# Adapter with layer norm: residual copied into PSUM by ScalarE, up-bias added by one product a tile

## What is computed

```python
h = x @ W_down[e] + b_down[e]        # 512x512 times 512x256
h = gelu(h)                          # exact gelu
h = h @ W_up[e] + b_up[e]            # 512x256 times 256x512
h = x + h                            # the residual
out = (h - mean) / sqrt(var + 1e-5) * ln_w[e] + ln_b[e]
```

## Time and profile before

| | |
|---|---|
| median of 3 runs | 68.33 us (67.98 to 68.78) |
| the profiled execution | 67.71 us |
| its span, first to last instruction | 65.8 us |
| TensorE busy | 57.7 us (88%) |
| VectorE busy | 49.6 us (75%) |
| ScalarE busy | 34.8 us (53%) |
| GpSimd busy | 40.3 us (61%) |
| DMA moved | 14.75 MB, mean 224 GB/s |

### The profile page before, as it was taken

How to read it: one execution, slowest core, us unless ns; L and a number is a source line. 1 busy time by engine, 2 the same in 40 slices (tenths; PEclk the granted TensorE clock), 3 DMA queues, 4 the chain that set the end, 5 groups by cost and what they waited for, 6 DMA issues and landing times. The chain is left out here.

```text
span 65.8 us, 975 instructions
## 1 busy us (share of the span) xinstructions
PE 57.7 (88%) x300; PEld 48.1 (73%) x300; DVE 49.6 (75%) x95; ACT 34.8 (53%) x51; POOL 40.3 (61%) x43
## 2 busy tenths in 40 slices
PE   0999999999999999999999999999999999990000
PEld 0999446898888888868888888888999898870000
DVE  0059912539999998969989894499999979999910
ACT  0700299987897559999940729991056204040000
POOL 4000070794999389999998999999199002327300
PEclk9999999999999999999999999999999999999996
DMA  0899897069999999999995074300000752400750
GB/s 0 319 329 309 309 351 289 10 173 420 274 354 416 423 411 339 414 415 411 413 426 217 17 306 179 157 10 0 0 0 0 319 214 105 159 0 0 258 194 26
DMA packets 4468, 14.75 MB, mean 224 GB/s; under 512 B 496, under 2 KB 496, under 8 KB 4464
## 3 DMA queue, kind: packets, MB, share of 16 engines
q1 hardware_dynamic: 4176, 13.65, 54.8%
q10 hardware_dynamic: 288, 1.05, 4.2%
HBM read 10.50 MB, written 4.19 MB: 223 GB/s over the span
## 5 line engine op out<-in xcount | busy, mean ns | idle before, releaser
L214 POOL TENSOR_TENSOR x_lo<-x_raw,x_hi 128x512 fp32r<-128x512 f32 x10 | 13.2, 1346 | 1.0 <-ACT x_hi L274 1.0
L535 PE MATMUL y_ps<-wu_hi,hid_hi 128*128 128x512 f32 x32 | 13.4, 418 | 0.0
L230 POOL TENSOR_TENSOR rstd<-var_eps,minus_half 128x2 f32<-128x2 f32 (+1 forms) x10 | 6.4, 639 | 10.5 <-DVE var_eps L373 10.5
L541 PE MATMUL y_ps<-wu_hi,hid_lo 128*128 128x512 f32 x32 | 12.7, 397 | 0.0
L537 PE MATMUL y_ps<-wu_lo,hid_hi 128*128 128x512 f32 x32 | 12.5, 392 | 0.0
L365 DVE BATCH_NORM_STATS2 stats<-y_ps 128x6 f32<-128x512 f32 x16 | 10.9, 691 | 2.1 <-PE y_ps L541 1.9
L225 POOL TENSOR_TENSOR wu_lo<-w_raw,wu_hi 128x512 fp32r<-128x512 f32 x8 | 10.4, 1321 | 2.1 <-ACT wu_hi L284 2.1
L382 DVE SCALAR_TENSOR_TENSOR y_ps<-y_ps,mean_var,ln_gb 128x512 f32<-128x512 f32 x16 | 11.5, 750 | 0.0
L392 DVE SCALAR_TENSOR_TENSOR result<-y_ps,rstd,ln_gb 128x512 f32<-128x512 f32 x15 | 10.8, 742 | 0.3
L292 ACT ACTIVATE x_res<-x_raw,w_raw 128x512 f32<-128x512 f32 x16 | 10.2, 711 | 0.0
L520 PE MATMUL y_ps<-ident,x_res 128*128 128x128 f32 x64 | 8.6, 272 | 0.0
(11 more groups left out here) (35 smaller groups left out, 87.4 us busy)
## 6 DMA issues: line engine op xcount, KB each, us to landing
x_raw<-x_cols SPq DMA_DIRECT2D x6, 512.0 KB, 7.7
out<-result SPq DMA_DIRECT2D x6, 512.0 KB, 3.0
w_raw<-weights SPq DMA_DIRECT2D x4, 512.0 KB, 7.4
ln_gb<-ln_rows SPq DMA_DIRECT2D x4, 512.0 KB, 12.5
w_raw<-weights SPq DMA_DIRECT2D x3, 516.0 KB, 8.8
x_raw<-x_cols ACTq DMA_DIRECT2D x2, 512.0 KB, 4.1
out<-result SPq DMA_DIRECT2D x4, 256.0 KB, 2.4
w_raw<-weights SPq DMA_DIRECT2D x1, 260.0 KB, 3.6
```

The source lines that it names most:

```text
L214: nc.gpsimd.tensor_tensor(x_lo[:, b % 2, k, :], x_raw[:, b, k, :], x_hi[:, b % 2, k, :].bitcast(F32), ALU.subtract).then_inc(x_lo_done, 1)
L535: nc.tensor.matmul(y_ps[:, t, :], hid_hi[:, p, j, rows], wu_hi[:, p, j, :], start=False, stop=False, skip_group_check=True)
L541: last = nc.tensor.matmul(y_ps[:, t, :], hid_lo[:, p, j, rows], wu_hi[:, p, j, :], start=False, stop=(j == JT - 1), skip_group_check=True)
```

## The change

In batches 1 to 3 the residual no longer goes through TensorE. x comes a second time, with tokens on the partitions (`x_rows`, 1 MB a batch), into the place where a batch's x before lay (`rows_of(b)` is `x_raw[:, b - 1]`), and ScalarE copies it tile by tile into `y_ps` (`copy_rows`), after VectorE's finish of the tile of the batch before. TensorE then waits for `copied`. Batch 0 keeps its way.

b_up is no longer added to x there. Its rows for batches 1 to 3 are loaded twice into partitions 0 to 2 and 3 to 5 of `bias_raw` (by SyncE, two rows of 2 KB each, three times). VectorE makes `bias_parts` of it once (`split_bias`): the rounded value in rows 0 to 2, what is left in rows 3 to 5. GpSimd builds `pick`, a matrix that is one in rows b - 1 and b + 2 for batch b, ScalarE rounds it (`pick_r`), and TensorE adds one product of 128 rows and 512 columns to each tile (12 in all).

```diff
+            def copy_rows(b, t):
+                act.wait_ge(rows_in[b], DMA)
+                act.wait_ge(norm_done, TT * (b - 1) + t + 1)
+                nc.scalar.activation(y_ps[:, t, :], rows_of(b)[:, t, :], ACT.Copy).then_inc(copied, 1)
...
+            def split_bias():
+
+                dve.wait_ge(bias_in, COPIED * DMA)
+                nc.vector.tensor_copy(bias_hi[:], bias_raw[:]).then_inc(bias_hi_done, 1)
+                dve.wait_ge(bias_hi_done, 1)
+                dve.wait_ge(mask_done, 1)
+                nc.vector.scalar_tensor_tensor(out=bias_parts[:], in0=bias_hi[:].bitcast(F32),
+                                               scalar=minus_if_low[:, 0:1], in1=bias_raw[:], op0=ALU.mult,
+                                               op1=ALU.add).then_inc(bias_parts_done, 1)
...
-            def up(b, t, j):
+            def up(b, t, j, low=True):
                 p = b % 2
                 rows = slice(t * P, (t + 1) * P)
                 n = JT * b + j + 1
+                if b and j == 0:
+
+                    pe.wait_ge(copied, TT * (b - 1) + t + 1)
...
+                if b and j == 0:
+                    if (b, t) == (1, 0):
+                        pe.wait_ge(pick_r_done, 1)
+                        pe.wait_ge(bias_parts_done, 1)
+                    nc.tensor.matmul(y_ps[:, t, :], pick_r[:, b - 1, :], bias_parts[:],
+                                     start=False, stop=False, skip_group_check=True)
...
+                if b == 0:
+                    for t in range(TT):
+                        place_residual(t)
+                up(b, 0, 0)
+                up(b, 1, 0)
+                up(b, 0, 1, low=False)
+                up(b, 1, 1, low=False)
+                up_low(b, 0, 1)
+                up_low(b, 1, 1)
```

More of the change, by code:

```diff
@@ L95, in conditional_adapter_kernel @@
         ln_in = [sem(f"ln_in{b}") for b in range(B)]
+        rows_in = [None] + [sem(f"rows_in{b}") for b in range(1, B)]
+        bias_in = sem("bias_in")
+        bias_filled = sem("bias_filled")
         stored = [[sem(f"stored{b}{c}") for c in range(2)] for b in range(LAST)]
@@ L181, in _ @@
             load_wu(0)
-            load_x(1, 0)
-            load_x(1, 1)
+            for b in range(1, 3):
+                load_x(b, 0)
+                load_x(b, 1)
             _, others = nc.values_load_multi_w_load_instructions(
@@ L186, in _ @@
             expert.extend(others)
-            for b in range(1, B):
[L188 to L195, removed]
+            load_wd(1)
+            load_wu(1)
+            load_ln(0)
+            load_wd(2)
+            load_rows(1)
+            for b in range(1, B):
+                load_bias(b)
+            load_wu(2)
+            load_ln(1)
+            load_x(3, 0)
+            load_x(3, 1)
+            load_rows(2)
+            load_wd(3)
+            load_wu(3)
+            load_ln(2)
+            load_ln(3)
+            store(0)
+            load_rows(LAST)
+            for b in range(1, LAST):
                 store(b)
@@ L317, in _ @@
                                  ACT.Copy).then_inc(first_wd_hi_done, 1)
-            residual(0)
+            residual()
             hi_wu(0)
@@ L402, in _ @@
             for b in range(LAST):
[L403 to L410, removed]
+                tile_stats(b, 0)
+                tile_stats(b, 1)
+                moments(b, 0)
+                moments(b, 1)
+                shift_var(b, 0, 2)
+                centre(b, 0)
+                centre(b, 1)
+                tile_stats(b, 2)
+                tile_stats(b, 3)
+                moments(b, 2)
+                moments(b, 3)
+                shift_var(b, 2, 4)
+                finish(b, 0)
+                finish(b, 1)
+                if b == 0:
+                    split_bias()
                 if b + 1 < LAST:
-                    finish(b, 0)
-                    finish(b, 1)
                     lo_hidden(b + 1, 0)
-                    finish(b, 2)
-                    finish(b, 3)
+                else:
+                    lo_hidden_half(0, 0)
+                    lo_hidden_half(0, 1)
+                centre(b, 2)
+                centre(b, 3)
+                finish(b, 2)
+                if b + 1 < LAST:
                     lo_hidden(b + 1, 1)
                 else:
[L419 to L423, removed]
                     lo_hidden_half(1, 0)
-                    finish(b, 3)
+                finish(b, 3)
             for t in range(TT):
```

117 lines of the change are left out of this document (85 added, 32 removed).

## The result

The changed kernel takes 70.62 us (median of 4 runs, 70.16 to 70.91); the kernel before took 68.20 us beside it (4 runs, 67.98 to 68.78). The ratio is 1.0335, with a 95% interval of 1.0248 to 1.0422: slower, by 2.4 us. The forecast was 69.5 us with a range of 67.5 to 71.2. The sign was right and the time lies in the range, but it lies above the span that the forecast gave itself (68.8 to 70.2). The loss is twice what the forecast had, and about half of it comes from a place where the forecast had nothing.

The account below looks back on a forecast made before the run. TensorE and VectorE were taken as nearly level, VectorE alone bounding the tail. Profiled: 67.71 + 2.1 (held split) - 0.8 - 0.1 (given back) = 68.9; as median 68.33 + 1.2 = 69.5 us, range 67.5 to 71.2.

Parts of the forecast that it names:

- held split: VectorE between batches 0 and 1: both split_bias instructions wait for GpSimd subtractions, batch 1's statistics start 2.1 us late.
- TensorE's part: Residual placement: 0.44 us a tile gives way to a 0.23 us bias product, saving 0.21 us a tile, 2.5 us in all.
- the tail: End of the last batch: VectorE has 9.77 us of its own work, so TensorE's savings there cannot move the end.
- ScalarE's part: Twelve copies into PSUM replace twelve residual activations at 0.65 us each; the new order hides the longer chain.
- rival of slow copies: ScalarE's copies into PSUM take 0.9 us or more, TensorE waits for `copied` every tile, past 70 us; chance 0.04.
- rival of the bare price: VectorE is not held in split_bias, which costs only its bare time: 67.6 to 68.4 us; chance 0.22.
- late-bias rival: Bias comes after 25.26 or x's rows late, split_bias misses a GpSimd boundary, term 3.4 us: 70.8 us; chance 0.26.
- The loads: SyncE's queue: W_down 1 goes out at 13.4, x 1's rows arrive at 24.7, the bias 24.8 to 25.2, just in time.
- the signs that the forecast named: Cast ending after a GpSimd subtraction, L486 1.5 us or more, `bias_parts` wait 1 us or more, statistics near 31.3 and 43.3.

Follow-up runs that it names:

- experiment 1: The kernel before with only the two loads of batch 2's x issued ahead of the expert-number load: 69.42 us, ratio 1.0150 to the kernel before.
- experiment 9: The changed kernel with split_bias's rounded copy written to PSUM instead of SBUF: 69.17 us, ratio 1.0135 to the kernel before.
- experiment 11: The changed kernel with all four expert numbers read at SyncE's start and the rounded bias written to PSUM: 68.53 us, ratio 1.0071 to the kernel before.
- experiment 6: The changed kernel with only all four expert numbers read at SyncE's start: 69.90 us, ratio 1.0298 to the kernel before.
- experiment 5: The changed kernel with expert numbers read at the start, bias loads and split_bias moved early, batch 2's x loaded later: 68.02 us, ratio 1.0019 to the kernel before.
- experiment 4: The kernel before with only the new instruction orders of VectorE and TensorE: 68.56 us, ratio 1.0032 to the kernel before.
- experiment 7: The kernel before with all four expert numbers read at SyncE's start: 68.86 us, too spread for a ratio.
- experiment 8: The kernel of experiment 5 with the next batch's W_down rounded behind the second gelu instead of ahead: 68.24 us, ratio 1.0054 to the kernel before.
- Experiment 12: The changed kernel with ScalarE reading the first expert number and issuing early loads, SyncE reading all four, rounded bias in PSUM: 67.97 us, runs 66.45 to 72.07.

## Why the prediction was right in sign and half in size

The ledger between medians: the kernel before 68.2; late loads about +1.2 (experiment 1); held split about +1.4 (experiments 9 and 11); together 70.8. Measured: 70.6. Everything else of the change (cheaper placements less the two bare instructions) comes out near nothing, -0.2 us, less than these runs can tell. The hold's share is measured in the changed kernel itself, twice. The share of the late loads is measured only by putting them into the kernel before; taking them out of the changed kernel (experiment 6) leaves their size open.

**TensorE's part, right in time, too large in busy time.** A tile's residual no longer takes TensorE's time, and the bias product is followed by the next after 0.23 us (31.36 to 31.59 below), as forecast. The timeline of TensorE's products in batch 1:

```profile
30.05 0.47 PE L642 MATMUL y_ps<-bias_parts,pick_r 128*128 128x512 f32 x1 [1.27 <-DVE bias_parts L486]
...
31.13 0.39 PE L636 MATMUL y_ps<-wu_lo,hid_hi 128*128 128x512 f32 x1
31.36 0.39 PE L642 MATMUL y_ps<-bias_parts,pick_r 128*128 128x512 f32 x1
31.59 0.39 PE L654 MATMUL y_ps<-wu_hi,hid_lo 128*128 128x512 f32 x1
```

The forecast gave back 0.8 us between the statistics of batches 1 and 2, and 0.1 behind; measured 0.81, then 0.21 and 0.11 (a total of 1.13 where 0.9 stood). The busy time fell by 1.8 us, not by the 2.5 forecast; no run says where the other 0.7 went. Most of TensorE's saving buys nothing, as the tail said: VectorE's last 9.77 us became 9.66.

**ScalarE's part, right.** The copies, whose price no row before showed, were put at 0.65 us. The page has them at 602 ns:

```profile
L366 ACT ACTIVATE y_ps<-x_raw 128x512 f32<-128x512 f32 x12 | 7.1, 602 | 4.1 <-DVE result L476 4.0
```

The rival of slow copies (0.04) falls. That the chain finish, copy, product costs nothing is borne out by experiment 5, which keeps it and is level with the kernel before; experiment 4 shows that the new orders alone cost nothing that can be told.

**The held split, right in mechanism and nearly in size.** The forecast gave 2.98 us from the end of the first finishes to the next low part (24.47 to 27.45) and 2.1 us at batch 1's statistics; measured 2.71 us (27.12 to 29.83) and 1.71. Both are 0.3 to 0.4 us below the forecast. Experiments 5 and 9 took the hold away, each in its own manner, and found 0.5 to 0.7 and 0.75 us for the two instructions. The Trainium skill, SBUF — State Buffer, "Who interferes with whom", had said that a cast too can be held; the trace of before did not show it, and now 1.10 and 1.12 us beside GpSimd against 0.42 to 0.43 alone do. The rival of the bare price (0.22) is refuted. The late-bias rival (0.26) had nearly the right time, 70.8, for a wrong reason: in the profile VectorE did not wait for the bias at all.

**The loads, the step that failed.** The forecast wrote: "their issue took 0.91 us, so W_down 1 goes out at 13.4 instead of 12.50". It went out at 15.12. Of the 2.62 us, the forecast had the 0.9; 0.4 more came from a later start and 1.3 from a longer read. The step treated the read of the expert numbers between x and W_down 1 as a fixed length. It was a variable one. Pointer and numbers together took 5.36 us before (4.97 in experiment 4, with the same loads ahead), 6.69 with another megabyte ahead (6.31 in experiment 1, 6.08 in experiment 9), and 2.26 in experiment 11, where they are read first. The forecast then priced the lateness only at the end of the queue (rows of x, bias), where slack took it up, and never asked who needs the loads just behind W_down 1. That was VectorE, for the layer-norm rows of batch 0. In the profile this is 1.54 us of wait. The rest of the 2.70 us before the centring (x of batch 1 a microsecond later with its cast held, and the variance instruction) is not shown to belong to the change: x of batch 1 came at 12.03 in experiment 4 and at 12.31 in experiment 7, which have no early load of batch 2, so the 11.17 of the profile before was early. Beside those two, whose centring starts at 21.51 and 21.52, the changed kernel's 22.75 is 1.2 us late, as much as experiment 1 measured.

The sum with this term mended: 2.1 + 1.2 (experiment 1) - 0.9 = +2.4 on 68.3, or 70.7, against 70.62. That it comes so near is in part luck: the split's term was 1.7 instead of 2.1 and the profiles gave back 1.13 instead of 0.9. Of the signs that the forecast named, the cast's end, the length of L486, the wait for `bias_parts` (1.3 us) and the tail came; the first statistics of batches 1 and 2 were to start near 31.3 and 43.3 and started at 33.66 and 45.59, which is where the missing term shows.

## What to carry to other kernels

A scalar read on a DMA-issuing queue has a length of its own, and here it ran from 2.3 to 6.7 us with what had been issued ahead of it: when loads move ahead of such a read, re-time it, then walk down the queue behind it and ask of each load who needs it first. On an engine without slack, price an added instruction that works in SBUF (a cast, or one with two inputs there) at what its like costs beside GpSimd's subtractions, not at its bare time; putting one operand into PSUM, or moving it to where the other engine rests, gives the difference back, but the second only if its data is there by then. And a saving on the busiest engine is worth only the waits of the others for it.

## What the runs showed of the hardware

SyncE's read of the expert numbers (pointer plus numbers) took 2.26 us at the very start (0.84 + 1.42, experiment 11), 4.97 to 5.36 behind batch 0's weights and x of batch 1 (experiment 4 and the kernel before), and 6.08 to 6.69 with x of batch 2 on top (experiments 9 and 1, the changed kernel). The pointer alone does not grow in such order: 3.97 before, and then 3.23, 3.97 and 5.16. I had taken the read as fixed.

A VectorE cast from SBUF to SBUF of 128x512 took 0.42 to 0.43 us alone and up to 1.33 us beside GpSimd's subtractions in the changed kernel (1.56 in experiment 8). Started during a subtraction, it ended 0.28 to 0.29 us after that subtraction's end, also when this was near (16.38 in the changed kernel, 9.82 in experiment 5). The same cast into PSUM took 0.68 us, and it took that in spite of GpSimd's work beside it (experiment 9).

Experiment 12 has the widest spread of all kernels here (66.45 to 72.07 us), with two queues issuing from the start. The cause stays open.
